# Norm roots of a windowed attention: one root write of 128 rows to DRAM, and a read-back that gathers each head's roots from four rows

## Chip, cores and metric

One core of a Trainium2 chip. The metric is device microseconds of one execution, median of the runs; here 3474.63 us for the kernel before (3 runs, 3473.0 to 3476.83). Less is better.

## What is computed

Eight sequences of 512 tokens of width 128 pass a linear-attention block (x + layernorm of it) and then six layers of local attention and a gated feed-forward. The change lies in the local attention, cut here to what matters (16 heads of 64, windows of 32 tokens):

```python
def l2norm(t):
    return t / jnp.maximum(jnp.linalg.norm(t, axis=-1, keepdims=True), 1e-12)
...
q, k, v = jnp.split(x @ Wqkv, 3, -1)          # per head: (b, 16, 512, 64)
q = l2norm(q) * qs
k = l2norm(k) * ksc
q = q * cos * scale + rotate_half(q) * sin * scale
k = k * cos * inv + rotate_half(k) * sin * inv
sim = jnp.einsum('bhwie,bhwje->bhwij', bq, bk2) * QK_SCALE   # 32 queries, 64 keys
attn = jax.nn.softmax(jnp.where(mask, -big, sim), -1)
out = jnp.einsum('bhwij,bhwje->bhwie', attn, bv2)
```

So each query and each key is divided by its norm. The kernel doesn't normalise before the rotation. It multiplies the rotated K by the reciprocal root of its squared norm (1/norm of each key), and gives the roots of Q to the exponential as its scale.

## The kernel before

**Units.** A unit u is one sequence in one layer (48 in all). It has 8 head pairs; n counts head pairs over all units (384), two heads of 64 on the two halves of the 128 partitions, tokens along the free dimension. m counts steps of two head pairs (192), q groups of four (96). The whole program is one list `o.line` of stages, sorted by the places of the table PLACE; each engine's program walks this list and issues the stages that are its own, so every engine and every queue runs strictly in this order.

**A head pair on its way.** PJ (TensorE) projects Q and K. PT (VectorE, L938) multiplies them by the rotary tables into TPB. TS (SyncE, L500) copies TPB with neighbouring partitions swapped into TR, two DMAs. AD (GpSimd, L1350) adds the two halves of the rotation into Q and K. PQ (ScalarE, L1221) squares the projections into SX, and SS (TensorE) sums the squares over the 64 dimensions of a head into a PSUM bank of 128 rows: row 32c + i holds the sums of the 128 tokens of quarter c for one of 16 rows i (a head pair gives two heads, Q and K; i is 0 to 7 for Q and 8 to 15 for K; rows 16 to 31 of each 32 are not used by RB). Eight SS stages, four head pairs, fill the bank once.

**The roots.** NM1 and NM2 (VectorE L946 to L955, ScalarE L1024 and L1026) make v to the power of -0.5, with a Newton step, in NV[:, 2, :], 128x128, once for each q. Their semaphore is nm_dve. Then the roots go two ways:
- RQ: TensorE transposes NV, and ScalarE copies the Q roots out as scales of the exponentials.
- RW (SyncE, L508) writes the K and Q roots to the DRAM tensor root_scratch, of which there are two, by q % 2; each is 16 rows of 512 tokens. RB (SyncE, L518) reads the row of a head, 512 roots, and spreads it over the 64 partitions of that head: two DMAs for each head pair into RB[n % 2]. PR (GpSimd, L1332) multiplies K by RB.

**Around it.** S1 (TensorE, scores K,Q of two head pairs) waits for `pr_pool` of both. MX, S3, SU, NP, TT (VectorE, ScalarE, GpSimd) are the softmax; PX and PY (SyncE, L524 to L534) put the transposed probabilities in place with six DMAs, and PV (TensorE) waits for them. On SyncE's queue the group in the steady state runs RW, PY, TS, RB, TS, RB, PX, PY, TS, RB, TS, RB, PX; a wait there holds everything behind it. The lines the change touches:

```python
elif st == "RW":
    ...
    on.wait_ge("nm_dve", 4 * q + 4)
...
elif st == "RB":
    ...
    on.wait_ge(f"rr_in{q % 2}", 64 * (q // 2) + 64)
    at = 8 + 4 * (n % 4 // 2) + n % 2
```

The other reader of the semaphore rr_in is ScalarE's NM1 of the next group, which must not overwrite NV before the write has read it. Other transfers that the prediction uses: the first stage's XIN (x in, 128x4x128 f32, L464), the copies of x1 to DRAM (L482, 128x512) and back (ER, L488, 128x512), and `out` (L492, 128x4x128).

Of the kernel before, what the change touches and what calls it, by code (L numbers as in the profile page):

```python
# [6 lines left out]
F32 = mybir.dt.float32  # L7
# [6 lines left out]
NB, L, D = 8, 512, 128  # L14
# [94 lines left out]
class Order:  # L109
# [27 lines left out]
    def no(self, stage, *key):  # L137
        return self.rank[stage, key]
# [168 lines left out]
def build(nc, xin, cst, awq, awk, awv, awo, wqkv, wo, w1, w2, vec, out):  # L307
    o = order()
    no = o.no
    with ExitStack() as ctx:  # L310
        def sb(name, shape, dt=F32, c=ctx):
            return c.enter_context(nc.sbuf_tensor(name, shape, dt))

        x1d = nc.dram_tensor("x1_scratch", (128, NB, L), F32, kind="Internal").ap()
        rootd = nc.dram_tensor("root_scratch", (2, 16, L), F32, kind="Internal").ap()
        PS = ctx.enter_context(nc.psum_tensor("PS", [128, 8, 512], F32))
        bank = [PS[:, i, :] for i in range(8)]
        X = sb("X", [128, NB, L + 1])
# [50 lines left out]
        NV = sb("NV", [128, 3, 128])  # L369
        RB = [sb(f"RB{i}", [128, L]) for i in range(2)]  # L370
# [33 lines left out]
        sem = Sems()  # L404
# [37 lines left out]
        def rq(m):  # L442
            return RQ[m // 2 % 2][:, m % 2, :]
# [5 lines left out]
        def sync_program(e):  # L449
            on = Waits(e)  # L450
            tab = CONST["tab"][0]
            e.dma_start(C[:, 0:tab], cst[:, 0:tab]).then_inc(sem["c_in"], 16)
            e.dma_start(T[2][:, :].rearrange("p (a d) -> p a d", a=4),
                        xin[0].rearrange("(a p) d -> p a d", p=128)).then_inc(sem["x_in"], 16)
            n_sel = CONST_COLS - KEPT
            e.dma_start(Vf[:, 0:n_sel], cst[:, KEPT:CONST_COLS]).then_inc(sem["sel_in"], 16)
            e.dma_start(WOA[:, :, :], awo.rearrange("p (c d) -> p c d", c=8)).then_inc(sem["awo_in"], 16)
            e.dma_start(VEC[:, :, :], vec).then_inc(sem["vec_in"], 16)
            e.dma_start(C[:, tab:KEPT], cst[:, tab:KEPT]).then_inc(sem["tab_in"], 16)
            for st, key in o.line:  # L460
                if st == "AL" and key[0]:
                    b, = key
                    on.wait_ge("al_pe", b)
                    e.dma_start(T[2][:, :].rearrange("p (a d) -> p a d", a=4),  # L464
                                xin[b].rearrange("(a p) d -> p a d", p=128)).then_inc(sem["x_in"], 16)
                elif st == "AG":
                    b, hp = key
                    g, half = 8 * b + hp, hp // 4
                    if g > 1:
                        on.wait_ge(f"qk_in{g % 2}", 128 * (g // 2))  # L470
                    if g > 5:
                        on.wait_ge("as_pe", 3 * g - 15)
                    for n in range(2):
                        on.wait_ge("aq_dve", no("AQ", b, half, n))
                        rows = slice(32 * (hp % 4), 32 * (hp % 4) + 32)
                        for c, low in enumerate(((0, 1, 0, 1), (0, 0, 1, 1))[n]):
                            e.dma_start((QA, KA)[n][c::4, g % 6, :].bitcast(F32),  # L477
                                        (TH, TL)[low][rows, n, half, :].bitcast(F32)).then_inc(sem[f"qk_in{g % 2}"], 16)
                elif st == "AZ":
                    b, = key  # L480
                    on.wait_ge("az_pool", b + 1)
                    e.dma_start(x1d[:, b, :], XR[b % 4][:, :]).then_inc(sem[f"x1_out{b}"], 16)  # L482
                elif st == "E1":
                    b, = key
                    on.wait_ge(f"x1_out{b}", 16)
                    if b:
                        on.wait_ge("e3_pe", b)
                    e.dma_start(ER[:, :], x1d[:, b, :]).then_inc(sem[f"x1_in{b % 2}"], 16)  # L488
                elif st == "E3":
                    b, = key  # L490
                    on.wait_ge("e3_act", b + 1)
                    e.dma_start(out[b].rearrange("(a p) d -> p a d", p=128),  # L492
                                EU[:, :].rearrange("p (a d) -> p a d", a=4)).then_inc(sem[f"y_out{b}"], 16)
                elif st == "TS":
                    n, = key
                    if n > 1:
                        on.wait_ge("ad_pool", 2 * n - 2)
                    on.wait_ge("pj_dve", 2 * n + 2)
                    for x in range(2):
                        e.dma_start(TR[n % 2][x::2, :, :], TPB[1 - x::2, 3 + n % 2, :, :]).then_inc(sem[f"t3_in{n % 2}"], 16)  # L500
                elif st == "RW":
                    q, = key
                    if q > 1:
                        for n in (4 * q - 6, 4 * q - 5):
                            on.wait_ge(f"rb_in{n % 2}", 32 * (n // 2) + 32)
                    on.wait_ge("nm_dve", 4 * q + 4)
                    for c in range(4):
                        e.dma_start(rootd[q % 2, :, 128 * c:128 * c + 128], NV[32 * c:32 * c + 16, 2, :]).then_inc(sem[f"rr_in{q % 2}"], 16)  # L508
                elif st == "RB":
                    n, = key  # L510
                    q = n // 4
                    if n > 1:
                        on.wait_ge("pr_pool", n - 1)
                    on.wait_ge(f"rr_in{q % 2}", 64 * (q // 2) + 64)
                    at = 8 + 4 * (n % 4 // 2) + n % 2
                    for s in range(2):
                        r = rootd[q % 2, at + 2 * s:at + 2 * s + 1, :]
                        e.dma_start(RB[n % 2][64 * s:64 * s + 64, :], r.broadcast_to([64, L])).then_inc(sem[f"rb_in{n % 2}"], 16)  # L518
                elif st == "PX":
                    m, = key  # L520
                    z = PP[m % 2]
                    on.wait_ge("tt_dve", 2 * m + 1)
                    for r in (0, 64):
                        e.dma_start(z[r:r + 32, 0, :, :], z[r:r + 32, 1, :, :]).then_inc(sem[f"po_in{m % 2}"], 16)  # L524
                    on.wait_ge("tt_dve", 2 * m + 2)
                    e.dma_start(z[32:64, 2, :, :], PX[64:96, :, :]).then_inc(sem[f"px_in{m % 2}"], 16)
                    e.dma_start(z[96:128, 2, :, :].rearrange("p (x c) a -> p x c a", c=4)[:, :, 0:3, :],
                                PX[0:32, :, :].rearrange("p (x c) a -> p x c a", c=4)[:, :, 1:4, :]).then_inc(sem[f"px_in{m % 2}"], 16)
                elif st == "PY":
                    m, = key  # L530
                    z = PP[m % 2]
                    on.wait_ge(f"po_in{m % 2}", 32 * (m // 2) + 32)
                    for r in (0, 64):
                        e.dma_start(z[r:r + 32, 1, :, :], PX[r + 32:r + 64, :, :]).then_inc(sem[f"px_in{m % 2}"], 16)  # L534
            for b in range(NB):
                on.wait_ge(f"y_out{b}", 16)
                on.wait_ge(f"x1_out{b}", 16)
# [480 lines left out]
        def scalar_program(e):  # L1018
            on = Waits(e)
# [19 lines left out]
            for st, key in o.line:  # L1039
                if st == "LW":  # L1040
                    i, = key
                    l, c = i // 12, i % 12
# [38 lines left out]
                elif st == "WC":  # L1081
                    i, = key
                    l, c = i // 12, i % 12
# [38 lines left out]
                elif st == "N1":  # L1122
                    kind, b = key
                    r = no(st, *key)
# [14 lines left out]
                elif st == "N3":  # L1139
                    kind, b = key  # L1140
# [12 lines left out]
                elif st == "AQa":  # L1153
                    b, half, n = key
# [5 lines left out]
                elif st == "AVa":  # L1160
                    b, i, n = key
# [7 lines left out]
                elif st == "ASa":  # L1169
                    t, = key  # L1170
                    n = (512, 384, 384)[t % 3]
# [5 lines left out]
                elif st == "AEa":  # L1177
                    b, hp = key
                    r = no(st, *key)
# [42 lines left out]
                elif st == "NM1":  # L1222
                    q, = key
                    if q:
                        on.wait_ge(f"rr_in{(q - 1) % 2}", 64 * ((q - 1) // 2) + 64)
                        on.wait_ge("rq_pe", q)
                    on.wait_ge("nm_dve", 4 * q + 1)
                    ln_exp(NV[:, 1, :], NV[:, 0, :], NV[:, 2, :], -0.5, "nm_act", q + 1)
                elif st == "VC":
                    j, = key  # L1230
                    u, hf, c = j // 8, j // 4 % 2, j % 4
# [4 lines left out]
                elif st == "S3":  # L1236
                    m, h = key
                    r, s = rq(m), h // 2
# [4 lines left out]
                    for g in range(4 * h, 4 * h + 4):  # L1243
                        at = 64 * (g - 8 * s)
                        p = e.activation(SC[m % 2][:, g, :, :].rearrange("p x k -> p (x k)"), bank[s][:, at:at + 64], ACT.Exp,  # L1245
                                         bias=BQ[m % 2][:, g:g + 1], scale=r[:, g:g + 1])
                    p.then_inc(sem["s3_act"], 1)
                elif st == "RQ":
                    q, = key
# [3 lines left out]
                elif st == "PVn":  # L1253
                    p, = key
# [18 lines left out]
                elif st == "F4g":  # L1273
                    u, i = key[0] // 3, key[0] % 3
                    l, n = u // NB, FP[i][1]
# [88 lines left out]
        @block.sync  # L1364
        def _(e):
            sync_program(e)
# [9 lines left out]
        @block.scalar  # L1376
        def _(e):
            scalar_program(e)
# [45 lines left out]
```

## Time and profile before

| | |
|---|---|
| median of 3 runs | 3474.63 us |
| profiled execution | 3475.88 us, of which the span of the instructions 3474.1 us |
| TensorE's granted clock | 0.979 of full |
| DMA | 447.01 MB, 129 GB/s over the span |
| DMA issues of the roots | 384 writes of 8 KB, 768 reads that write 128 KB each |

How to read it: the profile is one execution. Busy shares tell how full an engine is over the whole span; the chain of waits is followed back from the last instruction and tells which engines' work made up the time; a wait row tells which engine stood for which other's instruction, how long and how often. For a DMA there are two durations: that of the issue on the queue of the engine that starts it (SPq is SyncE's), and that from issue to landing. The share of the DMA queue in a stretch is the time of its packets over that of 16 DMA engines.

### The profile page before, as it was taken

To read this page: it belongs to the slowest core of one execution; us is meant where nothing else is said; L and a number is where in the kernel's file an instruction comes from. 1 tells how busy PE (TensorE), PEld (TensorE's weight loads), DVE (VectorE), ACT (ScalarE), POOL (GpSimd) and SP (SyncE) were. 2 spreads that over 40 slices of the span, in tenths; PEclk is the share of its full clock that TensorE was granted. 3 is DMA by queue.
4 is the path that set the end of the run, shared out by engine and by line. 5 is a ranking of instruction groups with operands and counts; after the bars stand their busy time and mean duration, and the time that the engine had idled before them with its cause. 6 is when DMAs were issued, how large, how long until landed. Compare 5 with 4: busy or idle time off the path is not lost.

```text
span 3474.1 us, 125058 instructions
## 1 busy us (share of the span) xinstructions
PE 3179.2 (92%) x52744; PEld 1975.5 (57%) x52744; DVE 2763.6 (80%) x3420; ACT 2536.5 (73%) x5866; POOL 2044.8 (59%) x1559
## 2 busy tenths in 40 slices
PE   7999997899999999999999899999999999999986
PEld 3444434566666566656666566666666665655553
DVE  3656657888888888888888888888888888888883
ACT  4666664778777777768787878787777777787784
POOL 0000006767677666767677777677767676766661
PEclk9999998999999999999999999999999999999998
DMA  3223324444444444444444444444444444434431
GB/s 110 77 75 80 80 57 135 140 142 136 145 149 145 135 134 145 144 140 137 140 136 148 138 151 138 140 141 152 146 142 137 134 146 139 143 127 145 137 130 31
DMA packets 271821, 447.01 MB, mean 129 GB/s; under 512 B 84254, under 2 KB 122396, under 8 KB 271132
## 3 DMA queue, kind: packets, MB, share of 16 engines
q1 hardware_dynamic: 244944, 422.50, 37.3%
q10 hardware_dynamic: 26316, 16.52, 1.7%
q8 instruction: 415, 6.80, 0.8%
q14 instruction: 146, 1.20, 0.1%
HBM read 124.21 MB, written 7.34 MB: 38 GB/s over the span
## 4 chain that ended last, share of the span: by engine, by line
PE 47%; DVE 24%; ACT 13%; issue 7%; SPq 3%; DMA 2%; POOL 2%; DVEq 0%; ACTq 0%; POOLq 0%
PE PS L542 47%; DVE TPB L938 8%; ACT SC L1245 8%; DVE SM L973 2%; DVE MX L962 2%; ACT SX L1221 2%; DMA RB<-root_scratch 2%; DVE NV L953 2%; DVE NV L951 1%; DVE PP L981 1%; POOL K L1332 1%; DVE H L1006 1%; SPq L477 1%; DVE NV L955 1%; ACT H L1024 1%
## 5 line engine op out<-in xcount | busy, mean ns | idle before, releaser
L938 DVE SCALAR_TENSOR_TENSOR TPB<-PS,VEC,C 128x1024 f32<-128x1024 f32 x768 | 959.1, 1269 | 98.7 <-ACT SX L1221 91.2
L1245 ACT ACTIVATE SC<-PS,BQ,RQ 128x64 f32<-128x64 f32 x3072 | 977.7, 437 | 40.0 <-DVE BQ L967 39.8
L1221 ACT ACTIVATE SX<-PS 128x512 f32<-128x512 f32 x768 | 468.6, 638 | 355.0 <-PE PS L542 347.9
L1332 POOL TENSOR_TENSOR K<-K,RB 128x512 f32<-128x512 f32 x384 | 496.2, 1292 | 286.8 <-DMA RB<-root_scratch 273.4
L1358 POOL TENSOR_TENSOR SC<-SC,RC 128x1024 f32<-128x1024 f32 x192 | 366.1, 1907 | 409.3 <-DVE RC L975 409.3
L542 PE MATMUL PS<-LXH,LH 128*128 128x512 f32 x768 | 379.2, 494 | 153.3 <-DVE TPB L938 145.9
L1350 POOL TENSOR_TENSOR K<-TPB,TR 128x512 f32<-128x512 f32 x384 | 499.2, 1300 | 0.0
L1350 POOL TENSOR_TENSOR Q<-TPB,TR 128x512 f32<-128x512 f32 x384 | 497.6, 1296 | 0.0
L542 PEld LDWEIGHTS PS<-PP,VV 64*64 64x64 f32 x12288 | 279.8, 136 | 149.7 <-issue 146.2
L542 PE MATMUL PS<-PP,VV 64*64 64x96 f32 (+1 forms) x12288 | 352.6, 250 | 4.3 <-DMA PP<-PX 2.0
L542 PE MATMUL PS<-AOT,LO 128*128 128x512 f32 x768 | 342.4, 599 | 0.0
L973 DVE TENSOR_REDUCE SM<-SC 128x16 f32<-128x1024 f32 x192 | 234.0, 1219 | 125.3 <-ACT SC L1245 123.8
L542 PE MATMUL PS<-K,Q 64*32 64x64 f32 (+1 forms) x24576 | 307.8, 225 | 26.8 <-issue 15.0
L542 PEld LDWEIGHTS PS<-LXH,LH 128*128 128x128 f32 x768 | 145.5, 189 | 313.1 <-DVE TPB L938 183.9
L542 PEld LDWEIGHTS PS<-K,Q 64*32 64x32 f32 x24576 | 293.0, 106 | 49.1 <-issue 19.9
L542 PE MATMUL PS<-LXH,LL 128*128 128x512 f32 x768 | 307.3, 400 | 0.0
L542 PE MATMUL PS<-LXL,LH 128*128 128x512 f32 x768 | 306.1, 399 | 0.0
L1235 ACT COPY VV<-PS 128x512 f32<-128x512 f32 x384 | 239.1, 623 | 89.2 <-PE PS L542 86.2
L542 PE MATMUL PS<-SX,C 128*32 128x128 f32 x6144 | 254.8, 283 | 2.2 <-issue 1.3
L542 PEld LDWEIGHTS PS<-AOT,LO 128*128 128x128 f32 x768 | 142.0, 190 | 170.4 <-issue 170.2
L962 DVE TENSOR_REDUCE MX<-PS 128x16 f32<-128x1024 f32 x192 | 233.2, 1214 | 5.6 <-PE PS L542 5.1
L1298 POOL TENSOR_TENSOR XR<-XR,T 128x512 f32<-128x512 f32 x8 | 10.2, 1276 | 365.6 <-DVE T L908 365.6
(166 smaller groups left out, 5862.8 us busy)
## 6 DMA issues: line engine op xcount, KB each, us to landing
TR<-TPB SPq DMA_DIRECT2D x768, 256.0 KB, 2.7
RB<-root_scratch SPq DMA_DIRECT2D x768, 128.0 KB, 3.0
PP<-PX SPq DMA_DIRECT2D x576, 64.0 KB
PP<-PP SPq DMA_DIRECT2D x384, 64.0 KB, 2.4
WS<-in_wqkv ACTq DMA_DIRECT2D x72, 128.0 KB, 2.5
PP<-PX SPq DMA_DIRECT2D x192, 48.0 KB
QA<-TH SPq DMA_DIRECT2D x128, 64.0 KB, 2.1
QA<-TL SPq DMA_DIRECT2D x128, 64.0 KB, 2.1
```

The costliest lines, as they stand in the source:

```text
L477: e.dma_start((QA, KA)[n][c::4, g % 6, :].bitcast(F32), (TH, TL)[low][rows, n, half, :].bitcast(F32)).then_inc(sem[f"qk_in{g % 2}"], 16)
L542: return e.matmul(dst, lhsT, rhs, start=start, stop=stop, **kw)
L938: e.scalar_tensor_tensor(TPB[:, n % 3:4 + n % 2:3 + n % 2 - n % 3, w, :], g, VEC[:, l, 9 + w:10 + w], C[:, at:at + 1024].rearrange("p (o c ...
L953: e.scalar_tensor_tensor(u, u, -0.5, x, ALU.mult, ALU.mult).then_inc(sem["nm_dve"], 1)
L962: e.tensor_reduce(MX[:, :], g, AX_X, ALU.max).then_inc(sem["s1_dve"], 1)
L973: e.tensor_reduce(SM[:, :], SC[m % 2][:, :, :, :].rearrange("p g x k -> p g (x k)"), AX_X, ALU.add).then_inc(sem["su_dve"], 1)
L1221: e.activation(SX[i % 3][:, :], bk("PJ", key)[:, :], ACT.Square).then_inc(sem["pj_act"], 1)
L1235: e.copy(VV[:, c, 512 * hf:512 * hf + 512], bk("VP", key)[:, :]).then_inc(sem["vp_act"], 1)
L1245: p = e.activation(SC[m % 2][:, g, :, :].rearrange("p x k -> p (x k)"), bank[s][:, at:at + 64], ACT.Exp, bias=BQ[m % 2][:, g:g + 1], scale ...
L1332: e.tensor_tensor(dst, dst, RB[n % 2][:, :], ALU.mult).then_inc(sem["pr_pool"], 1)
L1350: e.tensor_tensor((Q, K)[w][:, n % 8, :], TPB[:, n % 3, w, :], TR[n % 2][:, w, :], ALU.add).then_inc(sem["ad_pool"], 1)
L1358: e.tensor_tensor(sc, sc, RC[m % 2][:, :].rearrange("p (g o) -> p g o", o=1).broadcast_to([128, 16, 64]), ALU.mult).then_inc(sem["np_pool" ...
```

## The change

The root write becomes one DMA of all 128 partitions of NV, 512 bytes each, into a DRAM tensor of 128 rows of 128. The 512 roots of a head then lie in four rows, 32 apart, and each read-back takes them as four pieces of 512 bytes for each of 64 partitions. The semaphore counts 16 for each group in place of 64, in both places that wait for it. rr_in waits and everything else stay in their places; line numbers behind the write are one lower.

```diff
-        rootd = nc.dram_tensor("root_scratch", (2, 16, L), F32, kind="Internal").ap()
+        rootd = nc.dram_tensor("root_scratch", (2, 128, 128), F32, kind="Internal").ap()
...
                     on.wait_ge("nm_dve", 4 * q + 4)
-                    for c in range(4):
-                        e.dma_start(rootd[q % 2, :, 128 * c:128 * c + 128], NV[32 * c:32 * c + 16, 2, :]).then_inc(sem[f"rr_in{q % 2}"], 16)
+                    e.dma_start(rootd[q % 2], NV[:, 2, :]).then_inc(sem[f"rr_in{q % 2}"], 16)
...
-                    on.wait_ge(f"rr_in{q % 2}", 64 * (q // 2) + 64)
+                    on.wait_ge(f"rr_in{q % 2}", 16 * (q // 2) + 16)
                     at = 8 + 4 * (n % 4 // 2) + n % 2
                     for s in range(2):
-                        r = rootd[q % 2, at + 2 * s:at + 2 * s + 1, :]
-                        e.dma_start(RB[n % 2][64 * s:64 * s + 64, :], r.broadcast_to([64, L])).then_inc(sem[f"rb_in{n % 2}"], 16)
+                        r = rootd[q % 2, at + 2 * s::32, :].rearrange("(o c) d -> o c d", o=1).broadcast_to([64, 4, 128])
+                        e.dma_start(RB[n % 2][64 * s:64 * s + 64, :].rearrange("p (c d) -> p c d", c=4), r).then_inc(sem[f"rb_in{n % 2}"], 16)
...
                 elif st == "NM1":
                     q, = key
                     if q:
-                        on.wait_ge(f"rr_in{(q - 1) % 2}", 64 * ((q - 1) // 2) + 64)
+                        on.wait_ge(f"rr_in{(q - 1) % 2}", 16 * ((q - 1) // 2) + 16)
```

On SyncE's queue, the start of one group in the steady state (write, PY, TS and RB of two head pairs), before:

```order
L508 DMA root_scratch<-NV 16x128 x4
L534 DMA PP<-PX 32x512 x2
L500 DMA TR<-TPB 64x1024 x2
L518 DMA RB<-root_scratch 64x512 x2
L500 DMA TR<-TPB 64x1024 x2
L518 DMA RB<-root_scratch 64x512 x2
```

and the same place of the changed kernel:

```order
L507 DMA root_scratch<-NV 128x128
L533 DMA PP<-PX 32x512 x2
L500 DMA TR<-TPB 64x1024 x2
L517 DMA RB<-root_scratch 64x4x128 x2
L500 DMA TR<-TPB 64x1024 x2
L517 DMA RB<-root_scratch 64x4x128 x2
```

Nothing has moved: the write is one row in place of four, and the gathers have another shape. The other four engines run the same instructions in the same order.

## Rows read from the trace of the kernel before

**Rows 1.** Page, section 1: busy us, share of the span, instructions
```profile
PE 3179.2 (92%) x52744; PEld 1975.5 (57%) x52744; DVE 2763.6 (80%) x3420; ACT 2536.5 (73%) x5866; POOL 2044.8 (59%) x1559
```

**Rows 2.** Page, section 4: the chain that ended last, by engine
```profile
PE 47%; DVE 24%; ACT 13%; issue 7%; SPq 3%; DMA 2%; POOL 2%; DVEq 0%; ACTq 0%; POOLq 0%
```

**Rows 3.** The instructions on root_scratch: issue ns min/median/max; who waited
```profile
L518 SPq DMA_DIRECT2D RB<-root_scratch x768: 472/602/2205, 565.7 to 3386.0; - x192
L508 SPq DMA_DIRECT2D root_scratch<-NV x384: 302/420/708, 562.6 to 3373.3; - x192
...
  POOL K L1332: 273.4, 155
```

**Rows 4.** Waits of weight loads for GpSimd's K: us, times, longest
```profile
PEld PS L542 <- POOL K L1332: 16.7, 18, 2.6
```

**Rows 5.** The chain of waits, 2055 to 2071 us: start, us, what
```profile
2055.49 0.31 SPq L508
...
2057.23 0.55 SPq L534
...
2060.37 4.79 DMA RB<-root_scratch
...
2070.37 12.24 PE PS L542 x152
```

**Rows 6.** The write of x1 and the 32x4x96 form of PP, by line
```profile
L482 SPq DMA_DIRECT2D x_scratch<-XR x8: 325/344/348, 141.7 to 558.0; - x8
...
L527 SPq DMA_DIRECT2D PP<-PX x192: 632/637/1676, 597.7 to 3421.5; - x192
```

**Rows 7.** DMA issues of the whole span: KB each, us to landing
```profile
RB<-root_scratch SPq DMA_DIRECT2D x768, 128.0 KB, 3.0
...
root_scratch<-NV SPq DMA_DIRECT2D x384, 8.0 KB, 1.4
...
XIN<-in_x SPq DMA_DIRECT2D x8, 256.0 KB, 3.1
...
ER<-x_scratch SPq DMA_DIRECT2D x8, 256.0 KB, 3.2
```

**Rows 8.** DMA queue of 3468:3474, 3436:3445, 200:220, 300:320: packets, MB, share
```profile
q1 hardware_dynamic: 528, 0.26, 13.7%
...
q1 hardware_dynamic: 672, 0.52, 19.9%
...
q1 hardware_dynamic: 1288, 1.83, 34.9%
...
q1 hardware_dynamic: 1476, 1.55, 29.8%
```

**Rows 9.** Weight loads of S1 in order of time; the bracket is the wait
```profile
576.78 1.35 PEld L542 LDWEIGHTS PS<-K,Q 64*32 64x32 f32 x124 [0.24 <-POOL K L1332]
...
601.87 1.30 PEld L542 LDWEIGHTS PS<-K,Q 64*32 64x32 f32 x128 [1.28 <-POOL K L1332]
...
628.28 1.80 PEld L542 LDWEIGHTS PS<-K,Q 64*32 64x32 f32 x128 [2.21 <-POOL K L1332]
...
653.68 1.37 PEld L542 LDWEIGHTS PS<-K,Q 64*32 64x32 f32 x128 [1.88 <-POOL K L1332]
...
1538.48 1.55 PEld L542 LDWEIGHTS PS<-K,Q 64*32 64x32 f32 x128 [2.56 <-POOL K L1332]
...
1949.49 0.61 PEld L542 LDWEIGHTS PS<-K,Q 64*32 64x32 f32 x58 [0.33 <-POOL K L1332]
...
2300.64 1.55 PEld L542 LDWEIGHTS PS<-K,Q 64*32 64x32 f32 x128 [0.18 <-POOL K L1332]
...
2954.49 1.39 PEld L542 LDWEIGHTS PS<-K,Q 64*32 64x32 f32 x128 [1.42 <-POOL K L1332]
```

**Rows 10.** Timeline of GpSimd and of TensorE near 3016 us
```profile
3014.88 1.29 POOL L1332 TENSOR_TENSOR K<-K,RB 128x512 f32<-128x512 f32 x1
...
3016.29 0.93 PE L542 MATMUL PS<-K,Q 64*32 64x32 f32 x76
```

## The prediction

> **What bounds the kernel now.** I read the page's busy shares first, then the chain of waits, then what TensorE waits for, then the path from the norm roots to the scores. The shares [rows 1] say that no engine is full: TensorE is busy for 92% of the span, VectorE for 80%, GpSimd for 59%. The chain [rows 2] says where the end is set: 47% of it is TensorE, 24% VectorE, while SyncE's queue has 3% and the DMA transfers 2%. So what the change touches is at most a few per cent of the chain.
>
> The path of a group of four head pairs is: VectorE finishes the roots in NV, SyncE issues the root write, then the PX transfers of PY, the swapped copies of TS, then the two gathers into RB; GpSimd multiplies K by RB, and the next S1 on TensorE needs that product for two head pairs. The 384 root writes make 96 groups, spread from 562.6 to 3373.3 us [rows 3], one in 29.6 us. GpSimd waits much for these gathers, 273 us in 155 places [rows 3], but it has slack. TensorE's weight loads wait for GpSimd's product only 18 times, 16.7 us in all [rows 4]. This is the sum that bounds the gain: a root path that is shorter can give back no more than TensorE waits for it, unless it also frees somebody else.
>
> One such place in full is [rows 5]: the first of the four writes is issued at 2055.49 us, PY follows only at 2057.23, then come TS and RB, the gather takes 4.79 us from the issue to landing, and TensorE starts S1 at 2070.37. I followed the chain through the whole span in stretches of 100 us: it goes over the root write 14 times, 13 of them on to the gather and S1 (one near the end turns off to PX). These 13 are the places where the time can be moved.
>
> **The write.** Three of four issues go. From the first of four to the next DMA's issue is 2057.23 - 2055.49 = 1.74 us [rows 5]. What one issue of 128 rows costs is not in the trace; from below it is the first of today's four, 0.31 us, with the 128x512 write of x1 at 0.34 just above; from above it is the median of today's writes, 0.42 [rows 3, 5, 6]. I take the upper, with 0.04 us between instructions 0.46, since it is the same buffer and the same target. Gain: 1.74 - 0.46 = **1.28 us** for everything behind it on SyncE's queue (PY, TS, RB). The DMA engines move 128 pieces of 512 bytes in place of 64, at 26 ns a piece (below) 1.7 us more over 16 engines, 0.1 us, in a time when the queue has only begun: nothing. The write must have landed before RB is issued. It lands 1.4 us after its issue today [rows 7]; RB comes no sooner than 0.46 us and the four issues of PY and TS, some 2.4 us, so there is a margin of about 1.4 us even for a write that takes twice as long. ScalarE waits for the write too, before it overwrites NV, but 29.6 us later: nothing.
>
> **The gather.** Each of the 768 transfers now takes 256 pieces of 512 bytes where it took 64 rows of 2 KB. Its new cost is in no row, so I bound it by pieces of both sizes. The last transfer of the kernel is alone: `out`, 512 pieces of 512 bytes out of SBUF, 13.7% of 16 engines over 6 us = 13.2 us, 26 ns each. With ER beside it (128 rows of 2 KB from DRAM) the share is 19.9% over 9 us = 28.7 us, so ER takes 15.5 us, **121 ns a row**. Pieces of 512 bytes from DRAM are in XIN: the stretch at 200 us has 894 packets of 2 KB (1.83 MB) in 34.9% x 320 us = 111.7 us, 125 ns each with their completion writes; the stretch at 300 us takes 95.4 us, and its 1.55 MB are XIN's 512 pieces and 629 packets of 2 KB. 95.4 - 629 x 0.125 = 16.8 us, **33 ns a piece** [rows 8]. So a gather costs 256 x 33 = 8.4 us of one engine where it cost 64 x 121 = 7.7, over 16 engines 0.04 us more, 0.09 for the pair. The two ends are these: nothing more (XIN in 512 pieces lands in 3.1 us, ER in 128 rows of the same 256 KB in 3.2 [rows 7]), and four times as long (below, the third case). I take 0.09, which is nearest to the rows. The issue has one more dimension; the 32x4x96 form of PP costs 0.637 us where the gather costs 0.602 [rows 3, 6], 0.07 us for the pair. Altogether 0.16 us.
>
> The row of XIN speaks against a page of the Trainium skill, "DMA: Bandwidth & Descriptors". Its section "Measured (HBM→SBUF, 128 partitions, SWDGE, issued from GpSimd)" puts a small transfer's floor at about 10.5 ns a packet over all engines. As an estimate from that figure 192 more packets are 2.0 us more for each gather, and the change would lose. No term here uses it.
>
> **The sum.** At a place on the chain RB comes 1.28 - 0.16 = **1.1 us** sooner. The saving there is the smaller of this and TensorE's wait. All 18 waits are 16.7 us [rows 4]. Five are off these 13 places: 576.78, 628.28, 1949.49, 2300.64, 2954.49, together 4.4 us [rows 9] (at 628 the gather waited behind TS, which waited for VectorE; at 2954 GpSimd waited for VectorE). Of the rest three are longer than 1.1, at 601.87, 653.68 and 1538.48, by 2.4 us together. 16.7 - 4.4 - 2.4 = 9.9 us. The queue's slack elsewhere is no gain: at S1 after the other two head pairs no root write stands before it. About a fifth I take off, since VectorE and ScalarE join the chain soon after S1 and may not all be ready earlier: **8 us**. The profiled execution took 3475.88 us (span 3474.1), so 3467.9; it stands 1.25 us over the median of 3474.63, hence **3467 us** on the scale of the medians, 0.2% less, just about what a measurement of this kernel can tell from no change.
>
> **The other cases.**
> 1. *Absorbed.* TensorE starts S1 sooner and then waits for VectorE's products (TPB) or ScalarE's exponentials, which are as busy as before. For it: VectorE's 24% of the chain, and it is 80% busy. Against it: behind a crossing the chain stays on TensorE for about 12 us. Gain 0 to 6 us: 3472 us.
> 2. *More than the sum.* All 16.7 us of waits go and PV, which waits for PY, gains too: 3475.9 - 16.7 - 1.3 = 3458 us. It would need an issue near zero and every crossing on time. Little speaks for it.
> 3. *The gather goes by pieces, and the write's gain is lost.* Place: the RB transfer after a root write. If each piece took what a row takes now, a gather would need 256 x 121 ns / 16 = 1.94 us in place of 0.48, the pair 2.9 us more. RB would arrive 2.9 + 0.1 - 1.28 = 1.7 us later than today. It decides from 1.28 us on. S1 of the first half of a group has little slack: 26 of the 96 start within 0.2 us of the product's end, from the one at 576.78 to the one at 3016.29, where the product begins at 3014.88, takes 1.29 and S1 starts 0.12 us behind it [rows 9, 10]. 26 x 1.6 = 42 us: about 3517 us; a half of this growth is near 3480. For it: the engines are crowded in these bursts, the gather takes 4.79 us and not its median of 3.0 [rows 5, 7]. Against it: XIN. This is also where the skill's packet rule would lead.
> 4. *The change does not do what it says.* The instruction order of all engines stays as it is but for the three issues, so only an issue that grows with its rows could undo it: a 128-row write at 1.7 us would leave 3476 or a little more. The x1 write, with the same rows, takes 0.34 us; I count this under no change.
>
> **How the numbers follow.** The forecast has 0.42, more than the sum 0.03, absorbed with the fourth case 0.40, the gather's slower case 0.15. Faster by over 0.2% (under 3467.7) is the forecast and the second case, 0.45; within 0.2% 0.40; slower 0.15. The range starts at 3457, the second case, and ends at 3482, which holds the absorbed case, an exposed gather of a little over 1.3 us, and leaves out about 0.13 at the slow end and 0.03 below.
>
> **What would show it.** In the profile after: 96 root writes in place of 384, each near 0.4 us on SyncE's queue and the next DMA 0.4 to 0.5 us behind its start; SyncE's 768 gathers at 0.60 to 0.65 us, landing within 0.2 us of today's 3.0; the weight loads' wait for GpSimd's K down from 16.7 us to about 5; GpSimd's wait for RB down by up to 100 us without a gain of that size in the span; the DMA share of the middle up by a hundredth at most. I am wrong if the gathers land in over 4 us, if the single write costs over 1 us, or if TensorE's waits for K are gone and the span is the same: then the chain had a second path beside it.

## The result, and the profile after

The changed kernel takes 3598.16 us (median of 4 runs, 3593.11 to 3609.12) where the kernel before takes 3473.82 in the same comparison: a ratio of 1.036, interval 1.0331 to 1.0389. It is slower by 124 us, where 7.6 us less were forecast (3467 for 3474.63), and far above the 3482 us at which the forecast's range ends. The profiled execution took 3598.79 us, its span is 3597.0.

Page of the changed kernel, section 1 and section 4 (line numbers are one lower than before from the write on), against [rows 1, 2]:

```profile
PE 3215.2 (89%) x52744; PEld 1993.3 (55%) x52744; DVE 2783.7 (77%) x3420; ACT 2541.4 (71%) x5866; POOL 2079.6 (58%) x1559
...
PE 45%; DVE 21%; DMA 10%; ACT 9%; issue 7%; POOL 4%; SPq 4%; POOLq 0%; DVEq 0%; ACTq 0%
PE PS L541 44%; DVE TPB L937 8%; DMA RB<-root_scratch 7%; ACT SC L1244 3%; POOL K L1331 2%; SPq L500 2%; ACT SX L1220 2%; DMA PP<-PP 1%; DVE NV L954 1%; SPq L517 1%; DVE SM L972 1%; DVE NV L952 1%; DVE H L805 1%; DVE NV L950 1%; POOL Q L1349 1%
```

DMA has gone from 2% of the chain to 10%, the gather into RB alone has 7%, ScalarE and VectorE have less. The DMA view of the whole span (packets, MB and share of 16 engines, then KB each and median us from issue to landing), against [rows 7]:

```profile
q1 hardware_dynamic: 393936, 425.63, 39.7%
...
TR<-TPB SPq DMA_DIRECT2D x768, 256.0 KB, 3.6
RB<-root_scratch SPq DMA_DIRECT2D x768, 128.0 KB, 5.0
...
PP<-PP SPq DMA_DIRECT2D x384, 64.0 KB, 3.8
...
root_scratch<-NV SPq DMA_DIRECT2D x96, 64.0 KB, 1.6
...
XIN<-in_x SPq DMA_DIRECT2D x8, 256.0 KB, 3.0
...
ER<-x_scratch SPq DMA_DIRECT2D x8, 256.0 KB, 2.9
```

and the rows of the kernel before that answer to the first, second and fourth:

```profile
q1 hardware_dynamic: 244944, 422.50, 37.3%
...
TR<-TPB SPq DMA_DIRECT2D x768, 256.0 KB, 2.7
...
PP<-PP SPq DMA_DIRECT2D x384, 64.0 KB, 2.4
```

The gather lands in 5.0 us where it took 3.0. XIN and ER, in pieces of 512 bytes and in rows of 2 KB, stay at 3.0 and 2.9: pieces as such cost nothing in them. TS (TR, 2.7 before) and the first part of PX (PP<-PP, 2.4 before) land later too; both are issued behind gathers on the same queue. The engines are hardly busier: 37.3% of 3474.1 us before, 39.7% of 3597.0 now. The issues, against [rows 3] (ns minimum, median, maximum; us and times):

```profile
L517 SPq DMA_DIRECT2D RB<-root_scratch x768: 607/636/2377, 565.7 to 3508.7; - x192
L507 SPq DMA_DIRECT2D root_scratch<-NV x96: 320/326/711, 562.7 to 3494.8; - x96
...
  POOL K L1331: 644.7, 259
```

The write did a little better than was forecast: 96 issues of 0.33 us, where 0.42 was taken. GpSimd's wait for RB is up from 273 us to 645 [rows 3]. What waits for what, after (us, times, longest), against [rows 4]:

```profile
POOL K L1331 <- DMA RB<-root_scratch: 644.7, 259, 6.1
...
POOL SC L1357 <- DVE RC L974: 234.1, 91, 8.6
...
DVE X L990 <- PE PS L541: 160.7, 48, 7.0
...
PEld PS L541 <- POOL K L1331: 60.9, 46, 4.7
...
PE PS L541 <- POOL K L1331: 47.1, 41, 4.4
```

and the rows of the kernel before that answer to the second, fourth and fifth:

```profile
POOL SC L1358 <- DVE RC L975: 409.3, 101, 9.6
...
DVE X L991 <- PE PS L542: 90.4, 47, 6.8
...
PE PS L542 <- POOL K L1332: 11.3, 12, 2.3
```

TensorE's weight loads wait 60.9 us for the product of K where it was 16.7 [rows 4]. GpSimd waits 175 us less for VectorE's RC before it scales the probabilities (SC), which fits with its own work coming later; and VectorE waits 70 us more for the output projection that updates X.

Where the first gather goes is seen best at its first use, before the engines are crowded. In the stretch from 567 to 569 us (busy tenths of the DMA engines and GB/s, each in 40 slices of 0.05 us, then packets, MB and share), the kernel before:

```profile
DMA  0280537746247637485694635525231110000000
GB/s 0 41 205 0 164 123 246 246 164 164 82 164 246 205 123 246 164 287 205 246 369 164 246 123 205 205 82 205 82 123 41 41 41 0 0 0 0 0 0 0
DMA packets 169, 0.26 MB, mean 131 GB/s; under 512 B 41, under 2 KB 41, under 8 KB 169
...
q1 hardware_dynamic: 169, 0.26, 39.0%
```

and the changed kernel, with the same issues within 0.03 us:

```profile
DMA  0000202012121113311231121223312302311142
GB/s 0 0 0 10 61 31 61 31 41 51 41 51 51 31 31 72 51 31 41 41 51 41 31 51 51 61 31 51 41 31 61 51 31 41 51 41 41 31 41 51
DMA packets 173, 0.08 MB, mean 40 GB/s; under 512 B 16, under 2 KB 173, under 8 KB 173
...
q1 hardware_dynamic: 173, 0.08, 19.9%
```

Before, the pair of gathers moves 0.26 MB and is over at 568.7 us. Now 0.08 MB have moved in the 2 us, at some 45 GB/s, with the engines busy for a fifth: the rest of the time is not counted as their work, and the profile doesn't name what they wait for. The pair ends only near 571 us. It isn't slow all the way, though. The next 2 us, from 568.5 to 570.5 us:

```profile
GB/s 61 51 31 41 51 41 41 31 41 51 51 72 61 72 72 133 154 143 143 123 143 144 143 102 123 113 82 92 123 72 113 123 103 154 164 154 154 143 72 41
```

From 569.2 us on the same pair moves at 70 to 160 GB/s, with the second gather, issued behind the first, under way. So 45 GB/s is the rate of about the first 2 us. Why it rises is not shown.

### The profile page after: what moved, and what is told of

It reads as the page before. It is cut to its first block, busy times and chain, and to the rows that moved or that the text cites. A ratio compares the mean times of both kernels' runs of the same rounds, so it can differ in the third digit from the quotient of the medians.

```text
span 3597.0 us, 124770 instructions
## 1 busy us (share of the span) xinstructions
PE 3215.2 (89%) x52744; PEld 1993.3 (55%) x52744; DVE 2783.7 (77%) x3420; ACT 2541.4 (71%) x5866; POOL 2079.6 (58%) x1559
## 3 DMA queue, kind: packets, MB, share of 16 engines
q1 hardware_dynamic: 393936, 425.63, 39.7%
## 4 chain that ended last, share of the span: by engine, by line
PE 45%; DVE 21%; DMA 10%; ACT 9%; issue 7%; POOL 4%; SPq 4%; POOLq 0%; DVEq 0%; ACTq 0%
PE PS L541 44%; DVE TPB L937 8%; DMA RB<-root_scratch 7%; ACT SC L1244 3%; POOL K L1331 2%; SPq L500 2%; ACT SX L1220 2%; DMA PP<-PP 1%; DVE NV L954 1%; SPq L517 1%; DVE SM L972 1%; DVE NV L952 1%; DVE H L805 1%; DVE NV L950 1%; POOL Q L1349 1%
## 5 line engine op out<-in xcount | busy, mean ns | idle before, releaser
L1349 POOL TENSOR_TENSOR Q<-TPB,TR 128x512 f32<-128x512 f32 x384 | 514.0, 1339 | 0.0
L1349 POOL TENSOR_TENSOR K<-TPB,TR 128x512 f32<-128x512 f32 x384 | 512.5, 1335 | 0.0
L541 PE MATMUL PS<-PP,VV 64*64 64x96 f32 (+1 forms) x12288 | 364.2, 253 | 32.3 <-issue 26.7
L541 PEld LDWEIGHTS PS<-PP,VV 64*64 64x64 f32 x12288 | 287.4, 138 | 183.3 <-issue 173.5
L541 PE MATMUL PS<-K,Q 64*32 64x64 f32 (+1 forms) x24576 | 300.6, 226 | 58.6 <-POOL K L1331 47.1
L541 PEld LDWEIGHTS PS<-K,Q 64*32 64x32 f32 x24576 | 285.0, 106 | 87.5 <-POOL K L1331 60.9
L541 PE MATMUL PS<-SX,C 128*32 128x128 f32 x6144 | 265.0, 291 | 5.1 <-issue 3.1
```

What stands on the lines that cost most here:

```text
L541: return e.matmul(dst, lhsT, rhs, start=start, stop=stop, **kw)
L1349: e.tensor_tensor((Q, K)[w][:, n % 8, :], TPB[:, n % 3, w, :], TR[n % 2][:, w, :], ALU.add).then_inc(sem["ad_pool"], 1)
```

## The experiments

Three questions: is it the write or the gather; if the gather, is it the number of pieces or their addresses; and how does a later landing become 124 us. Ratios are to the kernel before on the same chip (medians 3477 to 3481 us there).

**The write alone.**

```diff
-r = rootd[q % 2, at + 2 * s::32, :].rearrange("(o c) d -> o c d", o=1).broadcast_to([64, 4, 128])
+r = rootd[q % 2].rearrange("(i c) d -> i (c d)", c=4)[8 * (n % 4) + 2 + s:8 * (n % 4) + 3 + s, :]
...
+e.dma_start(RB[n % 2][64 * s:64 * s + 64, :], r.broadcast_to([64, L])).then_inc(sem[f"rb_in{n % 2}"], 16)
```

> The single write of 128 rows as in the change, but each gather reads one contiguous row of 2 KB as before (of other heads: the roots that K is multiplied by are those of other tokens, so this run leaves the right scaling out). Theory 1 (the gather alone makes the loss): RB lands in 3.0 us at the median as before, the write is issued in 0.33 us, and the time is that of the sum of the prediction, 3463 to 3470 us. Theory 2 (the wider write takes part in the loss, by its landing of 1.6 us or its 64 KB): over 3480 us.

Measured: 3475.98 us, ratio 0.9988 (0.9976 to 0.9999); RB lands in 3.0 us. The write is no part of the loss. What it gives is 4 us, with an interval from nothing to 8, so the forecast of 8 us stands at its very edge. Its waits (us, times, longest):

```profile
POOL K L1331 <- DMA RB<-root_scratch: 268.7, 186, 4.1
PEld PS L541 <- DVE TPB L937: 234.0, 223, 3.1
...
ACT SC L1244 <- DVE BQ L966: 57.4, 60, 2.6
...
PEld PS L541 <- POOL K L1331: 2.2, 7, 0.5
```

The weight loads' wait for K, 16.7 us before [rows 4], is down to 2.2, as it should be with the write's three issues gone; their wait for VectorE's TPB is 234 us where it was 216, and ScalarE's for BQ 57 where it was 40. The wait that the sum counted was real, and at least a part of it was handed on to others. The write's issue there:

```profile
L507 SPq DMA_DIRECT2D root_scratch<-NV x96: 320/325/526, 562.8 to 3366.4; - x96
```

**The gather alone.** Four writes of 16 rows into the changed layout, the gather as in the change.

```diff
-e.dma_start(rootd[q % 2], NV[:, 2, :]).then_inc(sem[f"rr_in{q % 2}"], 16)
+for c in range(4):
+    e.dma_start(rootd[q % 2, 32 * c:32 * c + 16, :], NV[32 * c:32 * c + 16, 2, :]).then_inc(sem[f"rr_in{q % 2}"], 16)
```

> Four writes of 16 rows as before, into the rows of the changed layout, and the gather of four pieces as in the change. Theory 1 (the gather alone): landing of RB 5.0 us, and a time above that of the changed kernel by what three more issues cost, 3600 to 3615 us. Theory 2 (the write takes part): under 3590 us.

Measured: 3624.43 us, ratio 1.041 (1.0383 to 1.0437), RB 5.0 us. The whole loss is here, a little more than the 3600 to 3615 us expected. The four issues seem to cost more once the gather is late, 0.5% over the changed kernel against 0.1% without it, but the intervals touch.

**Pieces or addresses.** In this run K is multiplied by pieces of the x1 copy in DRAM, each partition's own: as many pieces of the same size, none repeated.

```diff
+on.wait_ge("x1_out0", 16)
...
+on.wait_ge("x1_out3", 16)
+r = x1d[64 * s:64 * s + 64, 0:4, 0:128]
```

> The changed kernel, but the gather takes its four pieces for each partition out of the x1 copy in DRAM: 256 pieces of 512 bytes as in the change, each at an address of its own and none repeated (K is multiplied by values of x1, so the scaling of K is left out). Theory P (pieces): landing 5 us, 3590 to 3605 us. Theory H (the repeated address): landing near 3 us, 3465 to 3500 us. In the first RB pair, near 566 us, theory P shows the same 45 GB/s, theory H over 200 GB/s.

Measured: 3480.71 us, ratio 0.9999 (0.9984 to 1.0014), RB 2.9 us. 256 pieces are as quick as 64 rows, so theory P falls. A partition of the x1 copy has 8x512 f32, 16 KB, so here it is the partitions that lie 16 KB apart, and the four pieces of each 2 KB. The second run puts the four pieces of a partition 128 KB apart, still each partition's own:

```diff
+for b in range(NB):
+    on.wait_ge(f"x1_out{b}", 16)
+r = x1d.rearrange("(c r) b l -> c (r b) l", r=8)[4 * s:4 * s + 4, :, 0:128].rearrange("c p l -> p c l")
```

> Pieces out of the x1 copy, each partition's own (2 KB from one partition to the next), but the four pieces of a partition 128 KB apart, a multiple of 16 KB (the scaling of K is left out again). Theory A1 (the step between the four is enough): RB lands in 4 us or later, 3540 us or more. Theory A with repetition (the step hurts only where all partitions ask for the same pieces): RB 2.9 to 3.2 us, 3470 to 3500 us.

Measured: 3484.32 us, ratio 1.0002 (0.9978 to 1.0026), RB 2.9 us. A step of 128 KB between the four is harmless where the partitions differ. Its stretch from 567 to 569 us, with the gathers issued at nearly the same time (0.15 us later):

```profile
DMA  0000000347546787876343667689756545321000
GB/s 0 0 0 0 0 0 20 102 143 225 154 143 184 236 266 236 246 215 174 92 143 113 195 205 205 195 236 246 236 164 195 164 133 143 82 62 41 21 20 10
DMA packets 546, 0.26 MB, mean 131 GB/s; under 512 B 34, under 2 KB 546, under 8 KB 546
...
q1 hardware_dynamic: 546, 0.26, 45.3%
```

All 512 pieces pass within the 2 us where the change moved 157. Both runs differ from the change in two things at once: no piece is repeated, and the pieces spread over more than one place of a 16 KB pattern, over four in the first run and eight in the second (steps of 2 KB between the pieces or the partitions). No run reads 256 different pieces at one place of that pattern, so whether repetition is needed for the loss is not shown.

**The step between repeated pieces.** Only the row pitch of the DRAM tensor is changed, and write and gather use the first 128 floats of each row: `(2, 128, 160)` for rows of 640 bytes, and 144, 256, 192 and 132 floats for the others, in the order of the texts.

> The changed kernel with rows of 640 bytes in DRAM, so that the four pieces of a head lie 20480 bytes apart and not 16384. Theory A (the loss is one of addresses: pieces 16 KB apart fall on the same part of the memory): RB lands near 3 us, and the time is 3470 to 3500 us. Theory P (it is one of pieces: 256 of them are issued or read one by one whatever their addresses) and theory H (64 partitions ask for the same 512 bytes): no change, landing 5 us, 3590 to 3605 us.

> The changed kernel with DRAM rows of 576 bytes: the four pieces lie 18432 bytes apart, that is 16 KB and 2 KB. Theory A (pieces that are all asked for by 64 partitions are slow where their addresses are a multiple of 16 KB apart): RB lands in 3.3 to 3.6 us like the 640-byte rows, 3485 to 3505 us. Rival A2 (the further from a power of two the better, 640 was good because of its 4 KB): between the two, 4 to 4.6 us and 3530 to 3570 us.

> DRAM rows of 1024 bytes: the pieces lie 32768 bytes apart. Theory A: as slow as the changed kernel or slower, RB 5 us or more and 3590 us or more. Theory A3 (only 640-byte rows differ because each row then lies in another page or part of its own, whatever the step): RB 3.5 us and about 3500 us.

> DRAM rows of 768 bytes: the step between the pieces is 24576 bytes, 16 KB and 8 KB, so that two of the four pieces share each place of a 16 KB pattern. Theory S and theory R both: between 16 KB and 18 KB steps, RB 3.6 to 4.4 us, 3500 to 3560 us. If what counts is only whether the step is an exact multiple of 16 KB: RB 3.0 to 3.5 us as with 576 and 640 bytes, under 3505 us.

> DRAM rows of 528 bytes, the step is 16 KB and 512 bytes, as if the four pieces lay side by side in a 16 KB pattern. Theory S: as 576 bytes, RB 3.0 to 3.2 us, 3470 to 3485 us. If the pattern is coarser than 512 bytes (pieces side by side still share a place): over 3.5 us, over 3500 us. It is also the candidate for the best version; beside the 576-byte rows it should not differ by over 0.2%.

Then two more layouts: four pieces side by side, 640 bytes apart (four writes, tensor `(2, 16, 4, 160)`), and all four pieces the same one (`rootd[q % 2, at + 2 * s:at + 2 * s + 1, :]`, repeated over 64 partitions and 4).

> Four writes as before, the four pieces of a head 640 bytes apart and side by side in DRAM, gathered as four pieces and repeated for 64 partitions. Against the run with four writes and pieces 16 KB apart (3624 us, RB 5.0 us) only the addresses differ. Theory A: RB lands in 3.0 to 3.6 us, 3475 to 3510 us. Theory H (the same 512 bytes for 64 partitions are slow in pieces, wherever they lie): over 4.5 us, over 3580 us.

> The changed kernel, but all four pieces of a partition are the same 512 bytes (step 0; the roots of the first quarter of the tokens are used for all four, so the scaling of K is partly left out). Theory S (one part of the memory serves all that is at one place of a 16 KB pattern, and its rate is the limit): as slow as the changed kernel or slower, RB 5 us or more, 3590 us or more. Theory R (pieces at different rows of one part of the memory disturb each other, while one row asked for again and again is quick): RB near 3 us, 3470 to 3500 us.

Measured, with the changed kernel among them (steps of 0, 24576 and 32768 have two runs each):

| step between the four pieces | RB landing, us: minimum, median | ratio | interval |
|---|---|---|---|
| 0, the same piece | 4.1, 5.0 | 1.0375 | 1.0332 to 1.0417 |
| 16384, the change | 4.1, 5.0 | 1.036 | 1.0331 to 1.0389 |
| 32768 | 3.1, 4.6 | 1.0224 | 1.0163 to 1.0285 |
| 24576 (16 KB + 8 KB) | 3.1, 4.7 | 1.0325 | 1.0283 to 1.0368 |
| 20480 (16 KB + 4 KB) | 3.1, 3.5 | 1.0056 | 1.0037 to 1.0075 |
| 18432 (16 KB + 2 KB) | 2.8, 3.0 | 0.9989 | 0.9968 to 1.0011 |
| 16896 (16 KB + 512) | 3.1, 3.8 | 1.0173 | 1.0141 to 1.0206 |
| 640, side by side (four writes) | 2.7, 3.1 | 1.0013 | 0.9992 to 1.0033 |
| a row of 2 KB (before) | 2.7, 3.0 | 1 | |

The last step of the reasoning is the first row: four pieces 16 KB apart behave to a tenth of a microsecond like one piece asked for 256 times. The landing of RB for the changed kernel, the same piece and the step of 18432 bytes:

```profile
DMA to landing us min/median/max: 4.1/5.0/7.5
...
DMA to landing us min/median/max: 4.1/5.0/7.8
...
DMA to landing us min/median/max: 2.8/3.0/4.9
```

So the loss is one of addresses. With 256 pieces in all, each asked for by 64 partitions or more, it is there at steps of 0 and 16384 bytes and gone at 640 and 18432, so repetition as such (theory H) falls, and pieces as such (theory P) with it. My theory that rows of one part disturb each other falls as well, since the same piece over and over is as slow. A pattern of exactly 16 KB is not borne out beyond these two steps. 32 KB is quicker than 16 KB and not as slow or slower; 16 KB + 8 KB is nearly as bad (4.7 us), where 3.6 to 4.4 was expected; and 16 KB + 4 KB is slower than 16 KB + 2 KB, where the same was expected. The 528-byte rows missed too: their pieces start at multiples of 16 bytes only, and the DMA share of the stretch from 700 to 3000 us is 0.52 where the 576-byte rows have 0.46, so other costs of that layout are mixed in; this was not taken apart. What in the memory makes a place is not shown by these runs.

The Trainium skill has a related measurement that the prediction overlooked: "DMA: Bandwidth & Descriptors", "Latency and other measured facts", reports copies between HBM tensors whose rate falls with a per-partition row pitch of large powers of two, from 207 GB/s at 512 KiB to 164 at 2 MiB and 103 at 4 and 8 MiB, and that 4 KiB of padding restores it, while 192 bytes did not. This case agrees that padding cures, with 2 KB in the step, but here 16 KB between pieces that 64 partitions repeat is enough, while 128 KB between pieces that differ from partition to partition cost nothing (1.0002).

**The price of a late gather.** The kernel before with eight writes of 8 rows.

```diff
-e.dma_start(rootd[q % 2, :, 128 * c:128 * c + 128], NV[32 * c:32 * c + 16, 2, :])
+for h in (0, 8):
+    e.dma_start(rootd[q % 2, h:h + 8, 128 * c:128 * c + 128], NV[32 * c + h:32 * c + h + 8, 2, :])
```

> The kernel before with eight writes of 8 rows in place of four of 16: whole rows are gathered as before, and the only change is that PY, TS and RB are issued about 1.8 us later after each root write. It measures the price of a late gather that the prediction's third case took as 26 places by 1.6 us: 42 us for 1.7 us. By that price: 3505 to 3550 us, ratio 1.010 to 1.022. Rival (a late gather alone costs nothing near that, since the group's other paths move along, and the loss of the change comes from the whole queue being slow): under 3495 us, ratio under 1.006.

Measured: 3516.09 us, ratio 1.0103 (1.0069 to 1.0137). The delay is smaller than I had meant, as an 8-row write is issued quicker. SyncE's queue, from the first write to PY:

```profile
2013.66 2.64 SPq L509 DMA_DIRECT2D root_scratch<-NV  x8
2016.34 1.19 SPq L536 DMA_DIRECT2D PP<-PX  x2
```

2.68 us where it was 1.74 [rows 5], so 0.94 us of delay cost 1.03%, 36 us. Weight loads then wait for K:

```profile
PEld PS L544 <- POOL K L1334: 48.5, 44, 2.6
```

that is 32 us more than [rows 4], as much as the profiled span has grown (3505.5 us where it was 3474.1). The slack is as thin on the slow side as the third case said, and thinner: it priced 1.7 us at 42, 25 us for each us of delay, where this run lost 38. TensorE's wait for K is not the only way to the end, though: the run with 640-byte rows lost 0.56% with 8.1 us of it, half of what the kernel before has.

**Which gathers hurt.** The kernel before, with the slow form (the same piece four times) for the first two head pairs of a group only, `n % 4 < 2`, and then for the last two only, `n % 4 > 1`.

> The kernel before, with the slow gather (four times the same piece, as in the run with step 0; so the scaling of K is partly left out) for the first two head pairs of each group of four, those that follow the root write. Theory 3 (the loss comes through S1 of the first step of a group, which has slack under 0.2 us in 26 of 96 places; by the run with the gather 0.94 us later 35 us): with 2 us later 80 to 120 us, ratio 1.023 to 1.035. Theory 4 (everything behind a slow gather on the same queue and on GpSimd is late, wherever it stands): half of the 143 us of the run with four writes and all gathers slow, ratio 1.016 to 1.024.

> The same with the slow gather for the last two head pairs of each group, whose S1 starts 2 us or more behind the product of K in the kernel before. Theory 3: under 0.6%, ratio 1.000 to 1.006. Theory 4: ratio 1.016 to 1.024, as much as the other half.

Measured: first half slow 3579.03 us, ratio 1.0292 (1.0255 to 1.0329); second half slow 3506.47 us, ratio 1.0081 (1.0053 to 1.0109). Weight loads' waits for K, first half slow:

```profile
PEld PS L546 <- POOL K L1336: 87.2, 51, 4.2
```

and second half slow:

```profile
PEld PS L546 <- POOL K L1336: 15.9, 17, 2.7
```

The slow half lands in 5.1 and 5.0 us, the other in 3.0 in both. The two halves together are 3.7%, nearly the 4.1% of the run with four writes and all gathers slow. So about seven tenths of that loss come through the step whose S1 stands right behind the root write (theory 3). The second half costs about 28 us without one microsecond more of TensorE's wait for K, a little over what theory 3 allowed: that part reaches the end by another way.

**TensorE's clock.** No run was made for it, but the traces show a part of the loss that no expectation named. The profiled span grew by 122.9 us. TensorE, with the same 52744 matmuls, is busy for 36.0 us more (3215.2 for 3179.2 [rows 1]) and does nothing for 86.9 us more. Its mean granted clock is

```profile
core 0: 3474.1 us, clock 0.979
...
core 0: 3597.0 us, clock 0.968
```

before and after, and 3179.2 x 0.979 / 0.968 = 3215.3: the lower clock alone gives the longer busy time. It falls behind waits. One of them in the changed kernel, then stretches of 4 us (us, TensorE busy, granted clock, DMA share, GB/s):

```profile
1448.10 0.80 PE L541 MATMUL PS<-LXH,LH 128*128 128x512 f32 x1 [2.68 <-DVE TPB L937]
...
1440.00:1444.00 4.00, 4.00 (x56) 1.00 0.40 72
...
1448.00:1452.00 4.00, 3.90 (x51) 0.50 0.50 173
1452.00:1456.00 4.00, 4.00 (x150) 0.74 0.25 62
1456.00:1460.00 4.00, 4.00 (x60) 1.00 0.41 150
```

TensorE is busy without a break, stands for 2.68 us, and then works at 0.50, the lower of its two levels (1.2 GHz), for 4 us and more. The kernel before does the same behind its longest wait for K: 0.50 from 1540 to 1544 us. Cut into stretches of 4 us from 560 us on, 32 of 729 lie below 0.8 before and 57 of 760 after. In the run with the second half slow it is 44 of 733, at a mean clock of 0.974: of the 16.1 us by which its profiled span (3490.2) is over that of the kernel before, TensorE is busy for 12.6 (3191.8 us). So most of what the second half costs in that execution, its quickest, is time at the lower clock. Which of its waits bring the clock down was not traced.

## Why the prediction was wrong

- **What bounds the kernel, and the root path in it: right.** The order write, PY, TS, RB, product, S1 is the path by which the time moved. But taking the 18 waits as the bound of the effect was right for a gain alone. The list of slacks in the third case said that lateness is dear, and the eight-write run shows it half as dear again.
- **The write: right** in its parts, a little too dear: 0.33 us for the issue (0.42 was taken), and no wait for the landing. Its gain, 8 us by the sum, measured 4 (0 to 8): the "fifth taken off" for VectorE and ScalarE was probably too little, and the first of the other cases (0 to 6 us) describes this run as well as the forecast does.
- **The gather: the step that failed.** "So a gather costs 256 x 33 = 8.4 us of one engine where it cost 64 x 121" reads a price out of XIN's pieces, each of which is read once from an address of its own. The nearest row by size and count was not the nearest by address: in RB 64 partitions ask for the same 512 bytes, and the change put the four pieces 16 KB apart. 0.04 us for each gather were forecast, 2.0 us measured; with the pieces 18432 bytes apart it is 0.0. The Trainium skill's price by packets, which the same part weighed, gives an estimate of 2.0 us as well (it was measured on transfers issued from GpSimd), but 256 pieces from addresses of their own land in 2.9 us, so the number of packets is not the cause.
- **The third case** named the right place and the right sign, with a chance of 0.15, and its mechanism (a piece costs as much as a row, by the count) was wrong: pieces are not slow in XIN or in the run with pieces of their own. Its price of 42 us, for a gather 1.7 us late, counted only the 26 places with under 0.2 us between the product's end and S1. In the same trace 50 of the 96 have less than 1.7 us, and what each lacks adds up to 64 us; counted so, 0.94 us of delay is an estimated 29 us (the profiled span of the eight-write run grew by 31) and 2 us of delay 80 us (the first half slow: 102). What it left out is shown in part: the second halves (0.8%), TS and the first part of PX, which land 0.9 and 1.4 us later, and TensorE's lower clock, 36 us of busy time in the profiled execution. The 124 us are not taken apart further.
- **The signs that were named** hold: I had written that gathers that land in over 4 us would prove it wrong; they land in 5.0.

## What to carry to other kernels

When a DMA repeats a source over many partitions and is cut into pieces, look at the step between the pieces before their count, and try a padded one: here 16 KB between them cost 3.6%, and 2 KB more in the step gave all of it back, while other steps (16 KB + 8 KB, 32 KB) did not. When a transfer's new cost is read from another row, compare size, count and addresses, repetition first. And a list of waits bounds only what a gain can give; for a loss look at how many places have no slack.

No version here beats both kernels clearly: the single write with 576-byte rows is level with the kernel before, 0.9989 (0.9968 to 1.0011), and it undoes all of the change's loss.

## What was not expected of the hardware

- Repeated pieces of 512 bytes come at some 45 GB/s for the first 2 us of a pair of gathers while the DMA engines show a fifth of their time as busy; the engines' share of the whole span, 39.7% where it was 37.3%, says little of such a limit.
- Steps of 0 and of 16384 bytes between four repeated pieces gave the same landing, 4.1 us at the least and 5.0 at the median, and 18432 bytes gave 2.8 and 3.0.
- A write of 128 rows is issued in 0.33 us, one of 16 rows in 0.42 at the median, one of 8 rows in 0.30: the issue does not grow with the rows.
- TensorE stood for 2.68 us and then had half its clock for 4 us and more: a wait was paid for again in the matmuls behind it.
